# Feed-forward score maxima: from a TensorE transpose and a VectorE addition to a VectorE block transpose and two DMAs through device memory, in a newly written order

## What is computed

```python
xn = _layernorm(x)
x = x + _L0_attn_ref(xn, W_qkv, W_out) + _L0_ffn_ref(xn, ...)
...
q = (x @ Wq + bq).reshape(B, S, H, Dh)          # H = 16, Dh = 8, no mask
k = (x @ Wk + bk).reshape(B, S, H, Dh)
v = (x @ Wv + bv).reshape(B, S, H, Dh)
scores = jnp.einsum('bqhd,bkhd->bhqk', q, k) / jnp.sqrt(jnp.float32(Dh))
attn = jax.nn.softmax(scores, axis=-1)
ctx = jnp.einsum('bhqk,bkhd->bqhd', attn, v).reshape(B, S, D)
x = x + layernorm(ctx @ Wo + bo, g1, be1)
...
moe_out = jnp.sum(top_vals[..., None] * picked, axis=2)
return x + layernorm(moe_out, g2, be2)
```

## Time and profile before

| what | us |
|---|---|
| median of 3 runs | 1200.87 |
| lowest and highest of them | 1196.76, 1202.64 |
| the profiled execution's own time | 1206.38 |
| its span in the trace | 1204.2 |
| TensorE (PE) busy | 1101.3 (91%) |
| VectorE (DVE) busy | 872.6 (72%) |
| ScalarE (ACT) busy | 829.0 (69%) |
| GpSimd (POOL) busy | 815.6 (68%) |

### The profile page before, as it was taken

One profiled execution on the slowest core, in us unless ns is written; L12 is line 12 of the kernel. 1 busy time (PEld: TensorE's weight loads), 2 busy tenths in 40 slices (PEclk: granted clock), 3 DMA queues, 4 the chain that ended last, 5 costly groups with the idle time before them and its releaser, 6 DMA issues.

```text
span 1204.2 us, 24802 instructions
## 1 busy us (share of the span) xinstructions
PE 1101.3 (91%) x8986; PEld 697.3 (58%) x8986; DVE 872.6 (72%) x2267; ACT 829.0 (69%) x1761; POOL 815.6 (68%) x753
## 2 busy tenths in 40 slices
PE   3789999999999998999999999999989999999996
PEld 2354566556565565656657566565566556565575
DVE  6577587866778667786787758787687876768657
ACT  3388777686666877578674886758766587666872
POOL 2666866587483977658874787766776678753980
PEclk9599999999799999999999999999999999799999
DMA  6111221112211221122210222112311122111110
GB/s 186 40 46 59 68 68 41 59 63 73 63 32 59 77 76 55 40 59 85 65 52 28 86 72 68 37 45 60 98 64 41 45 73 77 37 49 42 63 57 26
DMA packets 59621, 73.26 MB, mean 61 GB/s; under 512 B 17894, under 2 KB 29416, under 8 KB 59500
## 3 DMA queue, kind: packets, MB, share of 16 engines
q1 hardware_dynamic: 56028, 68.74, 18.3%
q10 hardware_dynamic: 3472, 2.95, 0.9%
HBM read 22.37 MB, written 3.15 MB: 21 GB/s over the span
## 4 chain that ended last, share of the span: by engine, by line
PE 66%; DVE 13%; ACT 8%; issue 4%; POOL 4%; DMA 3%; SPq 2%; ACTq 1%; POOLq 0%; DVEq 0%
PE work L1723 9%; PE work L1708 8%; PE work L1735 8%; PE work L1779 7%; DVE fnmax L1474 7%; PE work L1630 6%; PE work L1631 5%; PE work L1632 5%; PE work L1745 5%; PE work L1754 4%; ACT fpt L1312 4%; PE work L1769 3%; DVE work L1588 2%; ACT pn L1367 2%; PE work L1634 1%
## 5 line engine op out<-in xcount | busy, mean ns | idle before, releaser
L1474 DVE TENSOR_REDUCE fnmax<-work 128x2 f32<-128x1024 f32 x256 | 302.7, 1219 | 77.0 <-PE work L1754 76.1
L1209 POOL TENSOR_TENSOR raw<-raw,cos_t 128x512 f32<-128x512 f32 x128 | 164.0, 1281 | 259.4 <-DMA swapped<-raw 240.0
L1367 ACT ACTIVATE pn<-work,nmax 128x512 f32<-128x512 f32 (+3 forms) x512 | 264.8, 535 | 86.6 <-DVE nmax L1588 82.6
L1312 ACT ACTIVATE fpt<-work 128x1024 f32<-128x1024 f32 x256 | 250.8, 1025 | 74.0 <-PE work L1769 68.4
L1588 DVE CUSTOM_DVE_ANT_0 work<-work,causal 128x512 f32<-128x512 f32 (+3 forms) x512 | 237.0, 518 | 88.1 <-PE work L1708 87.7
L1723 PE MATMUL work<-consts,pn 128*128 128x128 f32 x1280 | 176.6, 284 | 12.1 <-DVE fnmax L1474 5.7
L1723 PEld LDWEIGHTS work<-consts,pn 128*128 128x128 f32 x1280 | 145.1, 144 | 50.4 <-DVE fnmax L1474 15.2
L1213 POOL TENSOR_TENSOR raw<-raw,swapped 128x512 f32<-128x512 f32 x128 | 163.7, 1279 | 10.0
L1224 POOL TENSOR_TENSOR qk_l<-raw,qk_h 128x512 fp32r<-128x512 f32 x128 | 163.1, 1283 | 2.9
L1210 POOL TENSOR_TENSOR swapped<-swapped,sin_t 128x512 f32<-128x512 f32 x128 | 164.0, 1282 | 0.0
L1379 ACT COPY pt<-work 128x1024 f32<-128x1024 f32 x128 | 128.5, 1020 | 43.5 <-PE work L1723 42.9
(11 more groups left out here) (155 smaller groups left out, 1857.7 us busy)
## 6 DMA issues: line engine op xcount, KB each, us to landing
swapped<-raw SPq DMA_DIRECT2D x256, 128.0 KB, 2.1
l_wide<-l_turned SPq DMA_DIRECT2D x128, 128.0 KB, 2.9
fqs<-fqn SPq DMA_DIRECT2D x96, 128.0 KB, 2.7
x_in<-in_L_attn_x_dram SPq DMA_DIRECT2D x8, 256.0 KB, 3.6
out_dram<-x_in SPq DMA_DIRECT2D x7, 256.0 KB, 2.9
fpt<-in_L_attn_W_qkv_dram ACTq DMA_DIRECT2D x3, 512.0 KB, 6.4
l_turned<-l_inv SPq DMA_DIRECT2D x64, 16.0 KB
pt<-in_L_ffn_We_dram ACTq DMA_DIRECT2D x1, 512.0 KB, 7.9
```

What stands on the lines that cost most here:

```text
L1209: nc.gpsimd.tensor_tensor(raw[:, n % 3], raw[:, n % 3], cos_t[:], ALU.mult)
L1312: nc.scalar.activation(fpt[:, ((b * G + g) * T + i) % FP, 2 * r:2 * r + 2].rearrange("p h n -> p (h n)"), bank_of(("fst", b, g, i), 2 * r, 2),
L1367: ins = nc.scalar.activation(pn[:, h, PN_AT[j]:PN_AT[j] + n], bank_of(("sc", b, c, unit), h)[:, at:at + n], ACT.Exp, scale=-1.0, bias=nmax ...
L1474: nc.vector.tensor_reduce(fnmax[:, j, 2 * r:2 * r + 2, 0:1], bank_of(("fsm", b, g, j), 2 * r, 2).rearrange("p (f n) -> p f n", f=2), AX.X, ...
```

## The change

`fmT` and `fsub` are gone, and so are `fqm` and a PSUM bank's use per group. `fnmax` shrinks to two copies of 128 x 32, with the 16 maxima columns of a group (4 query tiles x 4 heads) side by side. A new step `fturn` turns them by one VectorE transpose of 32x32 blocks. A new step `mput` writes the turned tile to a device-memory buffer `m_turned`, and a new step `mget` reads 16 of its rows (4 heads x 4 tiles x 128 queries) into row 0 of each strip of the queries in `fqs`. `fst` reads `fqs` itself. Since `fsm` needs that row to be zero, `fdup` gets a fourth DMA, issued first, that copies row 4 of each strip (zero) over row 0. Both tables are written anew, so every engine's order differs.

```diff
+        fnmax = sb("fnmax", [P, 2, STRIP], F32R)
-        fqm = sb("fqm", [P, S], F32R)
-        fnmax = sb("fnmax", [P, T, GH, STRIP])
+        m_turned = nc.dram_tensor("m_turned", [2, STRIP, P], F32, kind="Internal").ap()
...
                 elif kind == "fdup":
                     wait(sp, after("fst", *ring(2, b, g, G), T - 1))
+                    sp.dma_start(fqs[0:P:STRIP, g % 2, 0].bitcast(F32), fqs[4:P:STRIP, g % 2, 0].bitcast(F32)).then_inc(fdup_done[g % 2], 16)
...
+                elif kind == "mput":
+                    g = x_[2]
+                    wait(sp, after("fturn", b, g))
+                    wait(sp, landed("mget", *ring(2, b, g, G)))
+                    sp.dma_start(m_turned[g % 2].rearrange("c (a r) -> a c r", a=QUADS), fnmax[:, g % 2].bitcast(F32)).then_inc(mput_done[g % 2], 16)
+                elif kind == "mget":
+                    g = x_[2]
+                    wait(sp, landed("mput", b, g))
+                    sp.dma_start(fqs[0:P:STRIP, g % 2, 0].rearrange("f (t n) -> f t n", t=T).bitcast(F32),
+                                 m_turned[g % 2, 0:T * GH].rearrange("(t f) n -> f t n", f=GH)).then_inc(mget_done[g % 2], 16)
...
                     if j == 0:
-                        wait(dve, after("fmT", *ring(1, b, g, G)))
-                    nc.vector.tensor_reduce(fnmax[:, j, 2 * r:2 * r + 2, 0:1],
+                        wait(dve, landed("mput", *ring(2, b, g, G)))
+                    nc.vector.tensor_reduce(fnmax[:, g % 2, j * GH + 2 * r:j * GH + 2 * r + 2].unsqueeze(2),
                                             bank_of(("fsm", b, g, j), 2 * r, 2).rearrange("p (f n) -> p f n", f=2),
                                             AX.X, ALU.max, negate=True).then_inc(done["fmax"], 1)
-                elif kind == "fsub":
+                elif kind == "fturn":
                     g = x_[2]
-                    wait(dve, after("fmT", b, g))
-                    wait(dve, after("fst", *ring(1, b, g, G), T - 1))
-                    nc.vector.tensor_tensor(fqm[:], bank_of(("fmT", b, g)), fqs[:, g % 2, 0].bitcast(F32), ALU.add).then_inc(done["fsub"], 1)
+                    wait(dve, *(after("fmax", b, g, T - 1, r) for r in range(2)))
+                    nc.vector.transpose(fnmax[:, g % 2].bitcast(F32), fnmax[:, g % 2].bitcast(F32)).then_inc(done["fturn"], 1)
...
-                elif kind == "fmT":
-                    g = x_[2]
-                    wait(pe, *(after("fmax", b, g, j, r) for j in range(T) for r in range(2)))
-                    for t in range(T):
-                        ins = nc.tensor.transpose(psum[:, tile(t)], fnmax[:, t].rearrange("p h c -> p (h c)"), ident)
-                    ins.then_inc(done["fmT"], 1)
                 elif kind == "fst":
                     if i == 0:
-                        wait(pe, after("fsub", b, g))
+                        wait(pe, landed("mget", b, g))
...
-                        ins = nc.tensor.matmul(bank_of(x_, f), fqs[r, g % 2, 1, tile(i)], fqm[r], start=True, stop=True,
+                        ins = nc.tensor.matmul(bank_of(x_, f), fqs[r, g % 2, 1, tile(i)], fqs[r, g % 2, 0], start=True, stop=True,
...
     "xT": [
-        [85],
+        [83],
```

More of the change, by code:

```diff
@@ new lines @@
+    "v": [
+        [28, 32, 38, 43],
+        [165, 166, 173, 183],
+        [306, 307, 314, 323],
+        [447, 449, 455, 465],
+        [588, 590, 596, 606],
+        [729, 731, 737, 747],
+        [869, 871, 878, 888],
+        [1010, 1012, 1019, 1029],
+    ],
[9 rows of a table added]
+    ],
[9 rows of a table added]
+    ],
+    "fT": [
+        [53, 76, 96, 122],
+        [187, 218, 237, 263],
+        [328, 356, 379, 403],
+        [470, 499, 519, 542],
+        [610, 638, 662, 694],
+        [751, 780, 806, 830],
+        [892, 923, 942, 978],
+        [1033, 1057, 1083, 1103],
+    ],
[9 rows of a table added]
+    ],
@@ L243 @@
+        [291],
+        [432],
+        [573],
+        [714],
+        [855],
+        [998],
+        [1109],
     ],
     "x2T": [
[L245 to L252 removed]
+        [163],
+        [304],
+        [445],
+        [585],
+        [727],
+        [868],
+        [1009],
+        [1119],
     ],
     "gate": [
[L255 to L260 removed]
@@ L288 @@
         [3],
-        [80],
-        [199],
-        [329],
-        [459],
-        [587],
+        [81],
+        [200],
+        [337],
+        [462],
+        [588],
         [716],
-        [848],
+        [845],
     ],
     "fqkh": [
-        [4],
-        [88],
+        [6],
+        [87],
         [216],
         [344],
-        [474],
+        [473],
         [603],
-        [732],
+        [733],
         [860],
     ],
+    "raw": [
[8 rows of a table added]
+    ],
     "smh": [
-        [8],
+        [5],
+    ],
+    "weh": [
+        [10],
     ],
     "tab": [
-        [10],
-    ],
-    "raw": [
[8 rows of a table removed]
-    ],
-    "weh": [
         [9],
@@ L416 @@
         [912],
-        [1016],
+        [1015],
     ],
@@ L878 @@
+    "tp": [
+        "1316664244512060", "6402664233362400", "0560665224600340", "4616665124254040", "6402665134661360",
+        "6416665314460340", "6420665104660360", "0402661414464620",
+    ],
[8 rows of a table added]
 }
 ENGINE = {
-    "PE": ("tt", "tb", "xT", "fv", "fqk", "fsm", "fmT", "fst", "fpv", "fT", "cT", "wo", "x2T", "gate", "moe", "proj", "v", "sc", "tp",
+    "PE": ("tt", "tb", "xT", "fv", "fqk", "fsm", "fst", "fpv", "fT", "cT", "wo", "x2T", "gate", "moe", "proj", "v", "sc", "tp",
            "tq", "pv", "ao"),
@@ L886 @@
             "max", "tqe", "inv", "div", "yadd"),
     "POOL": ("rs0", "rs1", "rs2", "rope", "hi", "lo", "x2", "res", "out"),
-    "SP": ("swap", "lput", "lget", "fdup", "store", "load"),
+    "SP": ("swap", "lput", "lget", "fdup", "mput", "mget", "store", "load"),
 }
@@ L898 @@
         KEYS[kind] = [(c, unit, h) for c in range(NC) for unit in range(3) for h in range(2)]
-    elif kind in ("fT", "fdiv", "fdup", "fmT", "fo", "fsub"):
+    elif kind in ("fT", "fdiv", "fdup", "fo", "fturn", "mput", "mget"):
         KEYS[kind] = [(g,) for g in range(G)]
@@ L1053, in build @@
         lget_done = [sem(f"lget{n}_done") for n in range(2)]
+        mput_done = [sem(f"mput{n}_done") for n in range(2)]
+        mget_done = [sem(f"mget{n}_done") for n in range(2)]
         fdup_done = [sem(f"fdup{n}_done") for n in range(2)]
@@ L1085, in landed @@
         def landed(kind, *key):
-            sems, per, dmas = {"fdup": (fdup_done, G, 3), "lput": (lput_done, NC, 1), "lget": (lget_done, NC, 2)}[kind]
+            sems, per, dmas = {"fdup": (fdup_done, G, 4), "mput": (mput_done, G, 1), "mget": (mget_done, G, 1), "lput": (lput_done, NC, 1), "lget": (lget_done, NC, 2)}[kind]
             n = key[0] * per + key[1]
```

684 lines of the change are left out of this document (326 added, 358 removed), and 448 rows, old and new, of tables (PLACE, PSUM).

## The result

The changed kernel takes **1212.14 us** in the median of 13 executions (1203.53 to 1217.81), the one before 1198.34 beside it (1194.95 to 1202.64). The ratio is 1.0102, with a 95% interval of 1.0076 to 1.0128. I had forecast 1182 us, in a range of 1165 to 1206: the sign is wrong. A second set of 9 executions gave 1.0085 (1.0056 to 1.0114).

The account below looks back on a forecast made before the run. TensorE, 91% busy, was taken to set the pace. Transposes -16, earlier maxima -2, `fst` +3 and start -4 made -19 us against the profiled 1206.4, or 1182 us as the median runs 5.5 lower; range 1165 to 1206.

Parts of the forecast that it names:

- I let this term count in full.: On TensorE, 32 times four transposes go; as the pacing engine's work, all 16.0 us were to come off the time.
- the -2 of VectorE: TensorE's 23.2 us of waits for VectorE's maxima: 2 us credited because maxima are ready earlier; bounds nothing and 12 us.
- Rival 2: The gap stays and the work goes: TensorE waits longer for ScalarE's exponentials and VectorE's maxima, about 1200 us; chance 0.15.
- Its work as such is worth nothing: VectorE, 72% busy, has cover, so work taken from it brings nothing; only maxima ready earlier count.
- The new order was costed at nothing: The rewritten order of steps had no cost term of its own; its gain at the start was put at 4 us.
- The start, -4: First batch: six of group 1's maxima follow at once, bringing first causal scores forward by up to 6 us; 4 taken.
- The new way and its cover, 7.2 us under 7.7 to 9.1: Last `fsm` to landed read takes 7.2 us, hidden by TensorE's other work: 7.7 in group 0, 9.1 in group 3.
- The +3 charged for `fst`: `fst` of the eight groups 0, where cover is tightest: 3 us charged together; bounds nothing and 16 us.
- SyncE's queue at nothing: 96 added issues, 55 us, and up to 45 us of standing still on SyncE delay swaps, but were costed at nothing.
- rival 3: Slower, by SyncE's queue: first `fst` of groups 0 and 3 stalls about 2 us each, 1215 us; chance 0.13.
- The transposes' price: Four TensorE transposes taken at 0.50 us from the rows, 16.0 us in all; the skill's 55.6 ns would give 7 us.
- The sum: Whole kernel: -16 - 2 + 3 - 4 = -19 us against the profiled execution of 1206.4 us.

Follow-up runs that it names:

- old_none: Kernel before, in its own order, without the TensorE transposes and VectorE addition, maxima not subtracted: 1193.6 us, ratio 0.9947; again 1195.7 us, 0.9978.
- old_dve: Kernel before with feed-forward maxima taken over 474 of 512 keys of each head, so less VectorE work: 1190.0 us, ratio 0.9935.
- old_act: Kernel before with feed-forward exponentials of batches 1 to 7 over 936 of 1024 columns, so less ScalarE work: 1193.2 us, ratio 0.9965.
- new_none: Changed kernel without its three transfers per group, maxima not passed on: 1205.2 us, ratio 1.0040; again on another chip 1213.1 us, 1.0123.
- none_on: Changed kernel's source, maxima not passed on, with the old order up to batch 4, group 0, and the new order behind: 1210.1 us, ratio 1.0108.
- none_no: Changed kernel's source, maxima not passed on, with the new order up to batch 4, group 0, and the old order behind: 1194.0 us, ratio 0.9984.
- old_dma: Kernel before's order with the new way of the maxima put in, group 3's first `fst` moved behind one or two `fpv`: 1209.6 us, ratio 1.0092.
- old_pe2: Kernel before with each step of four TensorE transposes issued twice: 1205.6 us, ratio 1.0062.
- new_pe: Changed kernel's order with the old TensorE transposes and VectorE addition put in by hand: 1261.9 us, ratio 1.0511.

## Why the prediction was wrong

- **"I let this term count in full."** This step failed. The size of TensorE's work was somewhat too large: its busy time fell by 14.5 us, some 2 of them by the clock (0.963 against 0.961), so by about 12 us, where the forecast had 16.0 and its lower bound 13.1. Its worth was wrong: the -16 and the -2 of VectorE together measured -4.5 us (old_none), and TensorE's gaps grew by about as much as its work shrank. Busy 137.5 of 146 us looked like a pacing engine; old_dve and old_act show that VectorE and ScalarE are on the path too. Rival 2 had this mechanism, and I gave it 0.15.
- **"Its work as such is worth nothing"**, said of VectorE for its cover at 72% busy. This failed too: 20.1 us less of it gave 5.7 us (old_dve).
- **The new order was costed at nothing**, except for the gain at the start. This step failed too, and it made the sign: +11 us at one clock (new_none against old_none, each twice), all of it from batch 4 on (none_on, none_no). No rival had this cost either. I had worked out the order's cover for `fst`, and nowhere asked what the steps moved for it do to the waits elsewhere. none_no and none_on, with the same instructions in two mixed orders, differ by 13.7 us.
- **The start, -4.** Half right: the first `fst` comes later (36.2 against 34.9 us in the table), batch 0 is 3.5 us shorter, together -2.2. The six maxima follow at once, as forecast. The gain is part of the order's sum of +11.
- **The new way and its cover, 7.2 us under 7.7 to 9.1.** Right. Cover measured 8.7 and 9.4 us, write to read 2.3 us in group 3 and 2.0 in group 0, transpose 0.21, and the whole way from the last `fsm` to the landing 6.9 and 7.0 us. Groups 0 of batches 1 to 7 had a cover of 9.4 to 11.0 us, groups 3 of all batches 8.6 to 9.3. (Where the queue was busy, write to read went up to 3.8 us, in groups with more cover.) The read landed in 2.0 us where I had taken 2.5. The +3 charged for `fst` measured about +1 for everything that the transfers do. The Trainium skill (DMA: Bandwidth & Descriptors, the anatomy of one DMA) has some 2.0 us for a DMA's fixed cost, for DMAs that GpSimd issues; these are issued by SyncE, and the 2.0 us of their landings agree with the number.
- **SyncE's queue at nothing.** Right for this order, against its own sign: GpSimd's waits for swaps rose from 240 to 276 us, which I had named as a mark of rival 3. The kernel without swaps shows that such a wait can grow by 36 us and be worth nothing. Rival 3 had the right side of zero, and its 1215 us lie near the 1212 measured, by luck: its mechanism, `fst` standing for the read, did not occur. In the old order (old_dma) the transfers do cost 17 us.
- **The transposes' price.** The Trainium skill (TensorE: Matmul & The Clock Gate) would have had the saving at 7 us by its 55.6 ns. In old_pe2, 128 more transposes added 14.4 us of busy time, 0.11 us each, and cost 9 to 11: for their length the rows were the better guide.
- **The sum.** -4.5 + 11 + 1 = +7.5 us where I had -19. The changed kernel also runs at a lower mean clock, 0.967 against 0.972, another 4 us by the slope. That makes 12 us, as far as the means are apart (1210.1 and 1198.3); the medians are 14 us apart.

**Open** stays why the new order is level in batches 1 to 3 and loses in 4 to 6, though its pattern looks the same there; I did not splice at single steps. The new tables also give the steps other PSUM banks, and the splices change both at once, so how much of the 11 us is the banks is not shown. Nor is it shown how much of the 17 us of old_dma is my placing. Whether the lower clock comes from the gaps was not tried either.

## What to carry to other kernels

A busy share of 91% doesn't make an engine's work worth its length. Where several engines at 70% feed it in a fixed order, take the same time off each of them in turn and measure what comes back, before counting a saving in full. When a change comes with a new order of steps, measure the order alone, with the new and the old mechanism both left out: here that one pair of kernels gave the term that made the sign. And a wait that grows is no cost until removing it is shown to pay: look whether it stands in the part of the program that lost the time.

## What was not expected of the hardware

- Executions of one kernel differ in mean granted clock (0.962 to 0.982 for the kernel before, 118 executions), and this explains most of their differences: 0.86 us per 0.001. With the clock taken out, differences of 2 us could be read that the medians hid; new_none's two medians differ by 7.9 us, its times at one clock by 1.2.
- The clock may go with the kernel. Kernels with the new order in the second half ran at 0.965 to 0.970 (new_pe 0.957), those with the old order there at 0.969 to 0.976, highest with *more* TensorE work (old_pe2, 0.976). The two ranges touch, and new_none alone had 0.970 on one chip and 0.965 on another, so part of this may be chance.
